# Folding a query's norm into the exponential, and letting TensorE add the two rotary parts

## The reference, cut to what matters

```
q, k, v = split(shift_token(x) @ wqkv)           # 3 x 512 columns
q = l2norm(q) * qs ;  k = l2norm(k) * ksc        # each head of 64 to unit length
q = q * cos * scale + rotate_half(q) * sin * scale   # rotary position with xpos scale
k = k * cos / scale + rotate_half(k) * sin / scale
sim  = 8 * q @ k.T   over the own window and the one before, masked
out  = softmax(sim) @ v ;  x = x + out @ wo ;  then a gated feed-forward
```

## Time and profile before

| What | Value |
|---|---|
| Median of 3 runs | 2643.84 us (2635.1 to 2647.67) |
| The profiled execution's own time | 2645.18 us |
| Its span, first to last instruction | 2643.1 us |
| Mean granted TensorE clock | 0.845 of full speed |
| PE busy | 2017.8 us (76%) |
| DVE busy | 1314.4 us (50%) |
| ACT busy | 1241.3 us (47%) |
| POOL busy | 592.8 us (22%) |

### The profile page before, as it was taken

One profiled execution on the slowest core, in us unless ns is written; L12 is line 12 of the kernel. 1 busy time (PEld: TensorE's weight loads), 2 busy tenths in 40 slices (PEclk: granted clock), 3 DMA queues, 4 the chain that ended last, 5 costly groups with the idle time before them and its releaser, 6 DMA issues.

```text
span 2643.1 us, 38819 instructions
## 1 busy us (share of the span) xinstructions
PE 2017.8 (76%) x14843; PEld 1256.7 (48%) x14843; DVE 1314.4 (50%) x2660; ACT 1241.3 (47%) x2610; POOL 592.8 (22%) x505
## 2 busy tenths in 40 slices
PE   2865986489867987679868976788757999758776
PEld 1123664244344755333545754442345666535454
DVE  4134225654366145445654157734665545467574
ACT  2642421376644331667543333566645565235453
POOL 0420000263311001235400011433510221024231
PEclk8776995698978986888888987888978999778998
DMA  3000000000000100000000000000100110000000
GB/s 112 1 1 1 25 25 1 10 16 10 25 5 17 41 13 5 5 13 17 25 14 16 33 9 9 13 5 17 33 5 5 33 33 17 0 20 21 13 17 13
DMA packets 32059, 45.50 MB, mean 17 GB/s; under 512 B 7824, under 2 KB 18948, under 8 KB 31748
## 3 DMA queue, kind: packets, MB, share of 16 engines
q1 hardware_dynamic: 31875, 43.01, 6.0%
HBM read 24.12 MB, written 2.10 MB: 10 GB/s over the span
## 4 chain that ended last, share of the span: by engine, by line
PE 53%; DVE 25%; ACT 10%; issue 7%; POOL 4%; SPq 1%; DVEq 0%; DMA 0%; ACTq 0%; POOLq 0%
PE PH L933 8%; PE PD L893 8%; PE PH L716 5%; PE PB L1082 4%; PE PB L1102 4%; PE PB L1018 3%; ACT back_arena L1345 2%; PE PD L760 2%; PE PB L1039 2%; PE PB L1138 2%; POOL front_arena L1936 2%; ACT front_arena L1213 2%; DVE back_arena L1818 2%; DVE back_arena L1817 1%; PE PB L1029 1%
## 5 line engine op out<-in xcount | busy, mean ns | idle before, releaser
L1973 POOL TENSOR_TENSOR back_arena<-back_arena 128x512 f32<-128x512 f32 x128 | 165.4, 1294 | 1052.3 <-DVE back_arena L1818 1052.2
L1213 ACT ACTIVATE front_arena<-PD 128x1024 f32<-128x1024 f32 (+3 forms) x384 | 303.3, 817 | 160.7 <-PE PD L760 159.0
L1302 ACT ACTIVATE front_arena<-PD,b 128x512 f32<-128x512 f32 x256 | 161.6, 683 | 260.6 <-PE PD L893 260.4
L933 PEld LDWEIGHTS PH<-W,front_arena 128*128 128x128 f32 x2048 | 248.2, 192 | 65.6 <-issue 34.1
L1936 POOL TENSOR_TENSOR front_arena<-front_arena,tri 128x256 f32<-128x256 f32 x256 | 201.1, 798 | 322.4 <-ACT front_arena L1213 321.6
L933 PE MATMUL PH<-W,front_arena 128*128 128x128 f32 x2048 | 255.3, 276 | 7.6 <-DVE R L1664 6.7
L1082 PE MATMUL PB<-wqkv,hT 128*128 128x512 f32 x384 | 233.1, 696 | 32.5 <-DVE back_arena L1818 12.7
L893 PE MATMUL PD<-xT,W 128*128 128x512 f32 x512 | 246.4, 605 | 1.2 <-ACT xT L1196 1.2
L716 PE MATMUL PH<-front_arena 128*32 128x512 f32 (+3 forms) x1536 | 189.4, 569 | 66.2 <-POOL front_arena L1936 41.5
L1825 DVE TENSOR_REDUCE fnm<-PB 128x4 f32<-128x512 f32 x128 | 88.3, 691 | 303.6 <-PE PB L1102 302.0
L1345 ACT ACTIVATE back_arena<-PB,fnm 128x128 f32<-128x128 f32 x512 | 180.9, 371 | 111.0 <-DVE fnm L1825 110.8
(11 more groups left out here) (241 smaller groups left out, 3398.0 us busy)
## 6 DMA issues: line engine op xcount, KB each, us to landing
W<-in_W SPq DMA_DIRECT2D x32, 512.0 KB, 3.4
back_arena<-back_arena SPq DMA_DIRECT2D x128, 128.0 KB, 2.3
...
```

Source lines behind the costliest of these rows:

```text
L933: ins = pe.matmul(p[:, 128 * t:128 * t + 128], hv[:, c, 128 * t:128 * t + 128], W12[e % WRING][:, HF + 128 * c:HF + 128 * c + 128], start= ...
L1213: act.activation(pb[:, :, 0:n], p[:, :, 0:n], ACT.Exp, scale=INV_SQRT_HD).then_inc(freed(b, "S", half, g, kc, jp), 1)
L1973: pool.tensor_tensor(T1[k % 2][:, hs, :], T1[k % 2][:, hs, :], T2[:, hs, :], ALU.add).then_inc(sg("rot"), 1)
```

## The change

Three things are changed together. First, a query is no longer scaled to unit length. Its inverse norm is a factor per row of the scores, so it goes as `scale` into the exponential (one number per partition), and the row maximum is multiplied by it on DVE before it becomes the bias. `unit` scales the keys alone. Second, POOL no longer adds the query's two rotary parts. PE adds them: instead of a transpose, each of the four pieces gets two ordinary products with the identity, accumulated in PSUM. Third, `SQb` is halved: ACT's squares of k go where those of q were, so the sums of q's squares are taken separately on DVE (`squares_summed`), right behind the rotary of q, and ACT's square of k waits for it. `fy` gets three buffers and `T2` becomes one for k and two for q.

```diff
                 def turn_step(b, l, t, s):
                     k = (b * DEPTH + l) * NT + t
-                    pe.wait_ge(sg("unit"), k + 1)
+                    if s:
+                        pe.wait_ge(sg("unit"), k + 1)
+                    else:
+                        is_free(pe, b, "fq", l, t)
                     p = fill(pe, b, "ft", l, t, s)
                     for h in range(4):
                         c = 512 * s + 128 * h
-                        ins = pe.transpose(p[:, 128 * h:128 * h + 128],
-                                           T1[k % 2].rearrange("p a b -> p (a b)")[:, c:c + 128], ident[:, :])
+                        part = T1[k % 2].rearrange("p a b -> p (a b)")[:, c:c + 128]
+                        if s:
+                            ins = pe.transpose(p[:, 128 * h:128 * h + 128], part, ident[:, :])
+                        else:
+                            turn = T2q[k % 2].rearrange("p a b -> p (a b)")[:, c:c + 128]
+                            pe.matmul(p[:, 128 * h:128 * h + 128], part, ident[:, :], start=True, stop=False)
+                            ins = pe.matmul(p[:, 128 * h:128 * h + 128], turn, ident[:, :], start=False, stop=True)
...
                         ins = act.activation(fP[:, h, :], p[:, c:c + 128], ACT.Exp,
-                                             bias=fnm[:, h:h + 1], accum_out=fden[:, h:h + 1])
+                                             scale=fy[k % 3][:, 2 * (h - 4 * r) + r:2 * (h - 4 * r) + r + 1], bias=fnm[:, h:h + 1], accum_out=fden[:, h:h + 1])
...
-                    if k:
-                        act.wait_ge(sg("sums"), k)
-                    act.activation(SQb[:, 8 * s:8 * s + 8].rearrange("p a b -> p (a b)"), p, ACT.Square).then_inc(sg("squares"), 1)
+                    if k or s:
+                        act.wait_ge(sg("sums"), 2 * k + s)
+                    act.activation(SQb.rearrange("p a b -> p (a b)"), p, ACT.Square).then_inc(sg("squares"), 1)
...
-                    dve.tensor_reduce(fnm[:, 4 * r:4 * r + 4], p, AX, ALU.max, negate=True).then_inc(sg("largest"), 1)
+                    k = (b * DEPTH + l) * NT + t
+                    hs = slice(4 * r, 4 * r + 4)
+                    link(dve.tensor_reduce(fnm[:, hs], p, AX, ALU.max, negate=True))
+                    dve.wait_ge(sg("inverse"), k + 1)
+                    dve.tensor_tensor(fnm[:, hs], fnm[:, hs], fy[k % 3][:, r:NH:2], ALU.mult).then_inc(sg("largest"), 1)
...
-                    v = T1[k % 2]
-                    dve.tensor_tensor(v, v, fy[:, :].unsqueeze(2).to_broadcast([128, 16, DH]), ALU.mult).then_inc(sg("unit"), 1)
+                    v = T1[k % 2][:, NH:, :]
+                    dve.tensor_tensor(v, v, fy[k % 3][:, NH:].unsqueeze(2).to_broadcast([128, NH, DH]), ALU.mult).then_inc(sg("unit"), 1)
+
+                def squares_summed(b, l, t, s):
+                    k = (b * DEPTH + l) * NT + t
+                    dve.wait_ge(sg("squares"), 2 * k + 1 + s)
+                    dve.tensor_reduce(fss[:, NH * s:NH * s + NH], SQb, AX, ALU.add).then_inc(sg("sums"), 1)
...
                             rotary(b, l, i, 0)
+                            squares_summed(b, l, i, 0)
...
-                        for s in range(2):
-                            yield back_at(b, *((("k", l, t), ("t", l, t, 1) if turn else ("v", l, t))[s]))
-                            is_free(pool, b, "f" + "qk"[s], l, t)
-                            hs = slice(NH * s, NH * s + NH)
-                            pool.tensor_tensor(T1[k % 2][:, hs, :], T1[k % 2][:, hs, :], T2[:, hs, :], ALU.add).then_inc(sg("rot"), 1)
+                        yield back_at(b, *(("t", l, t, 1) if turn else ("v", l, t)))
+                        is_free(pool, b, "fk", l, t)
+                        keys = T1[k % 2][:, NH:, :]
+                        pool.tensor_tensor(keys, keys, T2k, ALU.add).then_inc(sg("rot"), 1)
```

26 lines of the change are left out of this document (13 added, 13 removed).

## The result

| | before | changed |
|---|---|---|
| Median | 2642.94 us (2635.1 to 2647.67, 4 runs) | 2665.1 us (2662.48 to 2666.81, 4 runs) |
| Span of the profiled execution | 2643.1 us | 2660.6 us |
| Mean granted clock | 0.845 | 0.874 |
| First projection of the last 16 tiles, from which the back runs alone | 2343.95 us | 2352.69 us |
| From there to the end | 299.2 us | 307.9 us |

The ratio is 1.0086 (95%: 1.006 to 1.0112): the changed kernel is slower by 22 us. Over all its runs the kernel before falls into two groups, 2631 to 2637 us at a mean clock near 0.850 and 2641 to 2652 near 0.845, of which the profiled execution belongs to the second, so ratios from different sets of runs can differ by some 0.3% for that alone.

What follows compares the result with a forecast made beforehand. No engine was taken to be full; the chain of waits runs through PE for 53%, DVE for 25%. Terms 35 + 11 - 7 - 6 - 6 - 5 = +22 us on 2645.2 gave 2667, put at 2666 us; forecast range 2650 to 2690.

Steps and rivals of the forecast that it cites:

- PE 35: Query's turn beside the front: products add 78 us over 48 tiles, 45% of it on the path, +35 us.
- clock -5: Whole kernel: PE's shorter waits bring a little more granted clock, -5 us (+5 to -15).
- POOL -6: Beside the front: POOL loses the query's addition, 61 us, letting causal masks through earlier, -6 us.
- back alone -6: Last 16 tiles: PE's path takes over, round falls to 11.3 us, -6 us (+10 to -13).
- Operand 11: Exponentials on ACT beside the front: second operand costs 0.08 us each, 31 us, 35% on the chain, +11 us.
- -7 for DVE: DVE beside the front: 0.76 us a tile less, 36 us, a fifth of it on the path, -7 us.
- rival 1: PE's products fall into its waits: 16 us for 35, ACT's term 5, total 2641 us, no change; chance 0.27.
- rival 2: DVE and POOL's loop sets the pace beside the front too: -29 us, 2616 us; chance 0.15.
- the term of 1.08 us: Softmax's multiplication on DVE: POOL's addition stretches 55% of them by 1.08 us; freeing softmax 0 gives -0.59 us a tile.
- I take nothing: ACT's square of k, bare in 16 rounds at layers' starts: counted as 0, 11 us if whole and on the path.
- Rival 3: Faster by the clock: mean grant 0.02 higher shortens PE's chain work by 33 us, 2639 us; chance 0.05.
- Rival 4: Much slower: PE's work paid like its average (54), ACT whole (31), bare waits (11), 2728 us; chance 0.08.

Runs made afterwards that it cites:

- e7: The kernel before with each query piece transposed four times over, sixteen transposes for four, nothing else changed: ratio 1.003.
- e8: The changed kernel without the norm: no scale in the exponential and no multiplication behind the maximum: ratio 0.9964.
- e2: The changed kernel with four transposes of the first rotary part in place of the eight products, second part left out: 1.0028, 2648.6 us.
- e3: The changed kernel with a constant scale of 0.01 in the exponential for the norm per partition, the maximum's multiplication kept: ratio 1.0081.
- e9: The changed kernel without the maximum's multiplication, and with a tile of ones as the exponential's scale per partition: ratio 1.0052.
- e4: The changed kernel with whole squares in a 16-bit buffer, one sum, and no wait of ACT's square of k: ratio 1.0077.
- e5: The changed kernel with sixteen transposes of the first rotary part in place of the eight products, second part left out: ratio 1.0102.

## Why the prediction was right, and where it was not

The total is right: +22.2 us measured, +22 forecast. The terms behind it are not all right: one was 22 us too high, two were 17 and 6 too low, and that they cancelled to a microsecond is luck. The experiments allow a sum in the forecast's own steps, from the kernel before to e7 (PE's occupation and the clock), from e7 to e8 (all that is taken off DVE and POOL, with the new wait), and from e8 to the changed kernel (the norm: the operand and the two multiplications).

| Step | Forecast, us | By medians, us | Beside the front / back alone, by the profiles |
|---|---|---|---|
| PE 35, clock -5 | 30 | 8 (5 to 11) | 7.0 / 0.4 |
| DVE without the multiplications -11, POOL -6, back alone -6 | -23 | -17 (-22 to -13) | -14.1 / -6.0 |
| Operand 11, multiplications 4 | 15 | 32 (24 to 40) | 15.9 / 14.3 |
| Sum | 22 | 23 | 8.8 / 8.7 |

The forecast's -7 for DVE is split here as it was made: 0.40 of its 0.76 us are the multiplications, with a sign against the rest: -1.16 x 48 / 5 = -11, and +0.40 x 48 / 5 = +4. The forecast's -6 for the back alone stands whole in the second line, though its path held 0.20 us for a multiplication.

**PE's products: mis-sized.** The step "I take 45%, nearer to the line's own bound: +35 us" failed. In e7 16 records cost 7 us beside the front with what the clock gives back, and between e2 and the changed kernel 1.3 there. What failed is the share, since the price of 1.27 us was right (1.86 us against some 0.65). Two things ate it. One is the clock, taken at -5 us without a row that priced it: at a grant of 1.00, which the records of the earlier trace rows had, 64 x 1.27 = 81 us were added, but PE's busy time rose by 2053.2 - 2017.8 = 35 us in e7 and by 32 in the changed kernel, so nearly 50 us of busy time came back. Windows of 1 us over the whole span show two levels of the grant: in the kernel before it was 0.50 in 754 of 2643 windows and 1.00 in 1755, in e7 0.50 in 638 of 2650 and 1.00 in 1890, with the rest in between. At 0.50 the same records took longer, from the first one's start to the last one's end: the changed kernel's eight products 3.75 us (from 1311.92 us) against 2.02 at 1.00 (from 2561.58 us), the kernel before's four transposes 1.06 us (from 1955.91 us) against 0.65 (from 621.36 us). The difference of products and transposes is thus 2.7 us at 0.50 and 1.4 at 1.00, where the forecast had 2.5 and 1.27. In the windows at 0.50 PE was busy for 465 us before and for 365 in e7. At the products' ratio, 3.75 / 2.02 = 1.86, these 100 us less would be 54 us at 1.00: an estimated 46 us of busy time given back, the 81 - 35 us that are missing in e7. The other is waits further on, as the 1.87 and 0.47 us in e7 show; the forecast's words against rival 1, "a wait ahead of an instruction covers nothing behind it", are true of the wait ahead, but the waits behind cover. For this term rival 1 (16 us for 35) was nearer than the forecast; that the total did not follow it is due to the norm. How the 7 us divide between clock and waits was not measured.

**What DVE and POOL were relieved of: right in kind and roughly in size.** POOL's 64 additions and softmax 0 at 0.69 us are as forecast, and -17 us stand against -23. So rival 2 did not fall for want of relief: e8 is 17 us faster than e7. The forecast called ACT's new wait covered in rounds with scores, though its own figures (1.5 us of exponentials against 1.2 + 0.6 us on DVE) leave 0.3 us bare; the trace has 0.30. A stretched multiplication ends 0.14 us sooner than the forecast's addition plus own time gives (2545.20 for 2543.38 + 1.27 + 0.69); the term of 1.08 us is not touched by that.

**The norm: mis-sized.** The forecast had the exponential's operand at 35% of its ACTIVATEs' work beside the front, and the multiplications at a fifth. Beside the front the two together came out as forecast in the one pair of profiles (15.9 for 15). In the back alone the forecast's path had 0.20 us for each multiplication and nothing for the operand, and there the two cost 14.3 us: 8.6 in the rounds, 2.9 in the change of layers and 2.9 behind the last maximum.

**The back alone: the step that failed outright.** "PE's path takes over, and the round is 11.3 us" rests on the time from `unit` to the end of rotary k, 5.25 us, which was the sum of DVE's instructions without a gap. That holds only as long as `unit` is late, as in the earlier trace rows. Once the power is no longer waited for, `unit` starts right behind largest 0, and two other paths lead from there to rotary q. One goes through largest 1, whose scores PE finishes 2556.32 - 2554.03 = 2.29 us after those of half 0. The other goes from largest 0 through its multiplication, four exponentials of half 0 and the square of q, both on ACT. Without the norm (e8) rotary q starts 2.90 us behind largest 0, by the first; with the multiplication alone (e3) it is 3.13, still by the first; with the operand alone (e9) the second takes over, and in the changed kernel it is 3.41. The forecast's path was carried to largest 0, and should have been carried on, by both ways, to rotary q. That the norm stands on it is shown (12.07, 12.31, 12.39 and 12.59 us for none, the multiplication, the operand, both). The 11.31 us of e2 are no support for the forecast, which had PE's products in a round of that length. Its shares of time at the lower level are in the trace of the kernel before: 28% beside the front (481 of 1863 windows of 1 us at 0.50, 82 in between) and 26% in the back alone (54 of 247, 18 in between). Its 1.9 us over before for a round at the lower clock was an estimate that no run shows: no round of the two layers ran at 0.50 throughout. The lowest mean grants of one are 0.63 in the kernel before, 13.34 us (from 2375.52 us) for the steady 12.38, and 0.87 in the changed one, 12.97 us (from 2407.67 us) for 12.59.

The steady round does not account for the 8.7 us by which the back alone grew, though. These are the windows of the kernel before, then of the changed one (columns as in the earlier trace rows): first layer from its first maximum to its last, the change to the second layer, the second layer, and what follows its last maximum.

```profile
2362.03:2453.84 91.81, 76.51 (x639) 50.12 (x641) 67.31 (x94) 51.77 (x176) 33.88 (x20) 0.83 0.09 20
2453.84:2498.74 44.90, 33.95 (x210) 20.24 (x211) 21.45 (x34) 19.57 (x42) 12.19 (x7) 0.92 0.06 13
2498.74:2592.12 93.38, 73.22 (x667) 50.25 (x669) 68.01 (x95) 52.56 (x178) 33.70 (x19) 0.93 0.08 18
2592.12:2643.10 50.98, 28.74 (x192) 18.76 (x192) 22.34 (x38) 12.34 (x31) 3.02 (x3) 0.82 0.05 11
```

```profile
2371.21:2460.73 89.52, 74.76 (x723) 53.57 (x724) 60.90 (x114) 57.12 (x175) 27.74 (x14) 0.98 0.09 22
2460.73:2511.42 50.69, 38.04 (x222) 22.64 (x223) 22.47 (x38) 20.30 (x44) 9.72 (x5) 0.87 0.05 11
2511.42:2606.70 95.28, 78.09 (x751) 56.42 (x753) 61.61 (x116) 57.43 (x176) 26.08 (x13) 0.98 0.08 18
2606.70:2660.60 53.90, 30.73 (x192) 19.80 (x192) 22.50 (x39) 13.27 (x33) 3.02 (x3) 0.79 0.04 11
```

The two layers together take 185.2 us before and 184.8 in the changed kernel, at a clock of 0.98 for 0.83 and 0.93. All the growth lies outside them: 0.4 us ahead of the first maximum, 5.8 in the change of layers, where the clock was 0.87 for 0.92, and 2.9 behind the last maximum, where it was 0.79 for 0.82. So the forecast's -6 us failed twice: its rounds gave 0.4 us, and for the rest of the back alone it had nothing where 9.1 were paid.

| Kernel | The two layers, us | Rest of the back alone, us |
|---|---|---|
| before | 185.2 | 114.0 |
| e7_before_sixteen | 183.9 | 115.7 |
| e8_no_multiplication | 176.2 | 117.4 |
| changed | 184.8 | 123.1 |
| e2_four_transposes | 172.4 | 124.3 |
| e4_whole_squares | 183.7 | 116.6 |

The forecast's "I take nothing" for ACT's bare waits at a layer's start falls in the change of layers. e4, without these waits, has 45.3 us there, but also a clock of 0.96. How much of the growth outside the two layers is the lower clock, and how much longer waits that came first, no run separates.

**The rivals.** Rival 1's 2641 us fell, on the norm. Rival 2, that DVE and POOL set the pace, has its own kernel in e8, at 0.9964, and its gain is 9 us against 29 forecast, without the norm. Rival 3's higher grant came and was larger (0.029, from 0.845 to 0.874) than the 0.02 it was costed at, with transposes (e5, e7) as with products; the gain in time did not: even e7, which changes nothing else, is slower than before. Rival 4 fell, and the new wait in it with e4.

**What stays open.** Singly, operand and multiplication cost nearly what both do together over the whole run, though in the steady round they nearly add up. Two paths that run side by side from the maxima (through DVE alone, and through ACT's exponentials) would do that, but no run separates them beside the front. Nor is it shown why e3 and e4 gain in the back alone and lose as much in front of it; single executions differ by some microseconds, so part of it may be scatter. No kernel with the whole computation was faster than the kernel before; the nearest is e7, which adds nothing useful. What e8 shows is that 9 us (6 to 13) would be there if the norm could enter at no cost on the path from the maximum to the exponentials.
